# Half-size first transfers and first norms, another order of scores 4 to 7, and a last result in three parts

## The reference, cut to what matters

```python
def _L0_xattn_ref(Q, K):                      # per sequence
    scores = jnp.einsum('btd,bsd->bts', K, K) * tril
    return Q + jnp.einsum('bts,bsd->btd', scores, Q)
def _L0_ffn_ref(x, ...):
    shared = silu(x @ shared_w1.T) @ shared_w2.T            # hidden 512
    gates  = softmax of the two largest of x @ gate_w.T     # 8 experts
    selected = sum over the chosen experts of gate * (silu(x @ w1_e.T) @ w2_e.T)
    return shared + selected
x = x + tanh(g_xattn) * _L0_xattn_ref(layernorm(x), ctx)
x = x + tanh(g_ffn)   * _L0_ffn_ref(layernorm(x), ...)
```

## Time and profile before

| What | Value |
|---|---|
| median of three runs | 228.3 us |
| profiled run | 228.44 us, span 226.6 us |
| PE busy (matmul) | 220.6 us, 97% of the span |
| PEld busy (weight load, beside PE) | 191.6 us, 85% |
| DVE (VectorE) | 118.0 us, 52% |
| ACT (ScalarE) | 133.0 us, 59% |
| POOL (GpSimd) | 147.6 us, 65% |
| chain that ended last | PE 90%, DMA 3%, DVE 2%, ACT 1%, POOL 1% |
| HBM | 30.45 MB read, 12.62 MB written |

### The profile page before, as it was taken

How to read it: one execution, slowest core, us unless ns; L and a number is a source line. 1 busy time by engine, 2 the same in 40 slices (tenths; PEclk the granted TensorE clock), 3 DMA queues, 4 the chain that set the end, 5 groups by cost and what they waited for, 6 DMA issues and landing times.

```text
span 226.6 us, 5999 instructions
## 1 busy us (share of the span) xinstructions
PE 220.6 (97%) x1728; PEld 191.6 (85%) x1731; DVE 118.0 (52%) x546; ACT 133.0 (59%) x304; POOL 147.6 (65%) x178
## 2 busy tenths in 40 slices
PE   7989999999999999999999999999999999999993
PEld 2754867786777789999999999999999999999793
DVE  6899998856864589995203210221122102466214
ACT  2649896597475555655565556545654565466510
POOL 4772875767777777777777777777744544465600
PEclk9999999999999999999999999999999999999998
DMA  6899210211245995867774266777777776999633
GB/s 233 263 392 392 66 54 33 64 52 52 68 98 156 260 285 161 228 185 183 197 202 151 72 196 202 215 238 223 219 244 220 200 228 187 271 355 370 238 95 127
DMA packets 30478, 43.47 MB, mean 192 GB/s; under 512 B 4992, under 2 KB 16512, under 8 KB 30192
## 3 DMA queue, kind: packets, MB, share of 16 engines
q1 hardware_dynamic: 25264, 32.87, 49.0%
q0 software_dynamic: 4320, 9.41, 11.4%
q10 hardware_dynamic: 864, 0.80, 1.0%
HBM read 30.45 MB, written 12.62 MB: 190 GB/s over the span
## 4 chain that ended last, share of the span: by engine, by line
PE 90%; DMA 3%; DVE 2%; ACT 1%; POOL 1%; issue 1%; POOLq 0%; SPq 0%; DVEq 0%; ACTq 0%
PE bank L1343 28%; PE bank L1364 28%; PE bank L1191 11%; PE bank L1204 10%; PE bank L1317 3%; PE bank L1138 3%; PE bank L1145 2%; DMA y_rows<-y,dest 2%; PE bank L1122 2%; PE bank L1211 2%; PE bank L1155 1%; DMA q<-y_rows 1%; PE bank L1115 1%; POOL rstd L492 0%; POOL y_rows L557 0%
## 5 line engine op out<-in xcount | busy, mean ns | idle before, releaser
L557 POOL DMA_INDIRECT y_rows<-y,dest x71 | 69.7, 982 | 36.6 <-ACT y L733 25.1
L531 POOL DMA_INDIRECT expert_rows<-n,slot x64 | 62.8, 981 | 24.3 <-issue 18.3
L1364 PE MATMUL bank<-w,hT 128*128 x568 | 74.5, 275 | 0.0
L1343 PE MATMUL bank<-xT,w_ring 128*128 128x128 f32 (+1 forms) x432 | 74.1, 309 | 0.0
L1364 PEld LDWEIGHTS bank<-w,hT 128*128 128x128 f32 x568 | 71.3, 192 | 1.6
L727 ACT ACTIVATE hT<-bank 128x512 f32<-128x512 f32 x71 | 42.4, 597 | 34.3 <-PE bank L1343 34.2
L1343 PEld LDWEIGHTS bank<-xT,w_ring 128*128 128x128 f32 x432 | 59.3, 192 | 2.0 <-issue 0.2
L1024 DVE COPY xT<-bank 128x512 f32<-128x512 f32 (+2 forms) x19 | 12.4, 653 | 72.3 <-PE bank L1317 72.3
L733 ACT ACTIVATE y<-bank,gate 128x128 f32<-128x128 f32 x71 | 26.1, 368 | 21.3 <-PE bank L1364 20.9
L1204 PEld LDWEIGHTS bank<-sw,sT 128*128 128x128 f32 x224 | 27.4, 192 | 5.3 <-issue 5.0
L1191 PE MATMUL bank<-nT,sw 128*128 128x512 f32 x56 | 28.7, 609 | 0.0
(11 more groups left out here) (154 smaller groups left out, 198.1 us busy)
## 6 DMA issues: line engine op xcount, KB each, us to landing
w_ring<-in_w1T SPq DMA_DIRECT2D x54, 256.0 KB, 3.6
x_ring<-expert_rows SPq DMA_DIRECT2D x37, 72.5 KB, 2.8
x_ring<-expert_rows SPq DMA_DIRECT2D x17, 145.0 KB, 3.7
w<-in_w2T SPq DMA_DIRECT2D x2, 1024.0 KB, 11.8
kT<-y_rows SPq DMA_DIRECT2D x8, 256.0 KB, 6.5
nT<-y_rows SPq DMA_DIRECT2D x7, 256.0 KB, 4.5
out<-xres SPq DMA_DIRECT2D x7, 256.0 KB
xres<-in_xP SPq DMA_DIRECT2D x3, 512.0 KB, 7.1
```

The source lines that it names most:

```text
L531: pool.indirect_dma_start(out=x_dram[:, :], out_offset=bass.IndirectOffsetOnAxis(ap=slot[:, i, k:k + 1], axis=0), in_=n[:, i, :], in_offse ...
L557: pool.indirect_dma_start(out=y_dram[:, :], out_offset=bass.IndirectOffsetOnAxis(ap=dest[:, b:b + 1], axis=0), in_=y[:, j], in_offset=None ...
L1343: last = pe.matmul(ps_up(b)[:, j * width:(j + 1) * width], w1_ring[:, w % W_RING, c * P:(c + 1) * P], xT[:, s % X_SETS, i * P:i * P + widt ...
L1364: last = pe.matmul(ps_y(b), hidden(b, c), w2[:, ds(at + c * D, D)], start=(c == 0), stop=(c == HC - 1))
```

## The change

It touches the first 25 us and the last 4 us of the timeline. It does this:

1. The first transfers are halved: tokens of group 0 on SP, context of group 0 on ScalarE (128 KB each). `statistics1(0)` and `score(0)` start on the first half and wait for the second at their third tile.
2. VectorE no longer clears `pad`; ScalarE does, in five activations (3 pad rows of 137 columns each) after its table load.
3. GpSimd makes the identity of the scores (`ident4`) first, and TensorE waits for that alone; `keep_warm(8)` becomes `keep_warm(6)`, and the one behind `transpose_n(0)` goes.
4. `norm1(0)` and `norm2(0)` (`first_norm`) run on two columns at a time, each half released to ScalarE by itself. The constants of `positions` are made before `norm2(0)`, the other routing constants behind `norm1(2)`.
5. Scores: banks 0, 4, 7, 5, 0, 7, 0, 4; scores 4 and 7 are copied instead of 4, 5 and 6. `score(4)` stands before `apply_scores(1)`, the tiles of `score(5)` between the transposes, `score(6)` behind them, `score(7)` between `shared_up(1)` and `apply_scores(2)`. `copy_scores(4)` stands before `normalise(0)`, `copy_scores(7)` behind `shared_silu(1)`. The context of group 7 is loaded ahead of the tokens of groups 4 and 5 and of `sw2`.
6. The last result comes in three parts, two tiles, one and one, from three banks, in three stores: the first by ScalarE, the others by SP.

```diff
-        ps_s = [bank[0], bank[4], bank[7], bank[5], bank[0], bank[7], bank[4], bank[7]]
-        COPIED = (4, 5, 6)
+        ps_s = [bank[0], bank[4], bank[7], bank[5], bank[0], bank[7], bank[0], bank[4]]
+        COPIED = (4, 7)
-        ps_last_sup, ps_last_so = [bank[1], bank[2], bank[5], bank[6]], [bank[1], bank[2]]
+        ps_last_sup, ps_last_so = [bank[1], bank[2], bank[5], bank[6]], [bank[1], bank[2], bank[5]]
+        def part_of(t):
+            return max(0, t - 1)
+        def part_cols(part):
+            return slice(0, 2 * D) if part == 0 else slice((part + 1) * D, (part + 2) * D)
+        def steps_to(g, half):
+            return g + 2 if g else half + 1
...
-            load_tokens(0)
+            sp.dma_start(xres[:, 0:GW // 2], xP[:, 0:GW // 2]).then_inc(x_first, 16)
+            sp.dma_start(xres[:, GW // 2:GW], xP[:, GW // 2:GW]).then_inc(x_in[0], 16)
...
             load_context(5)
+            load_context(6)
             load_tokens(3)
             sp.dma_start(sw2[:, :], sw2T).then_inc(sw2_in, 16)
-            load_context(6)
...
-            sp.wait_ge(last_added, 2)
-            sp.dma_start(outP[:, last_cols(1)], xres[:, last_cols(1)]).then_inc(stored, 16)
-            sp.wait_ge(stored, 16 * (GROUPS + 1))
+            for part in range(1, 3):
+                sp.wait_ge(last_added, part + 1)
+                sp.dma_start(outP[:, LAST * GW:][:, part_cols(part)], xres[:, LAST * GW:][:, part_cols(part)]).then_inc(stored, 16)
+            sp.wait_ge(stored, 16 * (GROUPS + 2))
...
+            chained(pool.memset(ident4[:, :, :], 0.0))
+            pool.affine_select(out=ident4[:, :, :], ...).then_inc(ident4_ready, 1)
...
+            def norm(slot_kind, done, some=slice(0, G)):
+                slot, kind = slot_kind
+                chained(pool.tensor_tensor(rstd[:, slot, kind, some], var_eps[:, slot, kind, some], minus_half[:, some], ALU.pow))
+                pool.tensor_tensor(shift[:, slot, kind, some], neg_mean[:, slot, kind, some], rstd[:, slot, kind, some],
+                                   ALU.mult).then_inc(done, 1)
+            def first_norm(slot_kind, stats_done, done):
+                pool.wait_ge(stats_done, 1)
+                for half in range(2):
+                    norm(slot_kind, done, slice(half * G // 2, (half + 1) * G // 2))
...
-            norm1(0)
+            first_norm(first(0), stats1_done, shift1_done)
             norm1(1)
+            position_constants()
+            first_norm(second(0), stats2_done, shift2_done)
+            norm1(2)
             routing_constants()
-            norm2(0)
-            norm1(2)
             norm1(3)
...
-            act.dma_start(kT[:, 0:GW], ctxT[:, 0:GW]).then_inc(ctx_in[0], 16)
+            act.dma_start(kT[:, 0:GW // 2], ctxT[:, 0:GW // 2]).then_inc(ctx_first, 16)
+            act.dma_start(kT[:, GW // 2:GW], ctxT[:, GW // 2:GW]).then_inc(ctx_in[0], 16)
             act.preload_act_table(ACT.Silu)
+            act.wait_ge(warm_ready, 1)
+            for i in range(0, PADS, PAD_ROWS):
+                act.activation(pad[:, i:i + PAD_ROWS, 0:AT], warm[...], ACT.Copy).then_inc(pad_zeroed, 1)
...
             centre_and_scale(1, 1)
+            copy_scores(4)
             normalise(0, 0)
...
             shared_silu(0)
-            copy_scores(4)
             centre_and_scale(3, 0)
-            copy_scores(5)
             shared_silu(1)
+            copy_scores(7)
             shared_silu(2)
-            copy_scores(6)
             shared_silu(3)
...
-            chained(dve.memset(pad[:, :, :], 0.0))
...
-            def add_last_shared(half):
+            def add_last_shared(part):
+                cols = part_cols(part)
+                dve.wait_ge(half_done, GROUPS + 1 + (part > 0))
+                dve.wait_ge(sdown_done, GROUPS + part)
...
-            keep_warm(8)
+            keep_warm(6)
             score(0)
             score(1)
             score(2)
             apply_scores(0)
             score(3)
+            score(4)
             apply_scores(1)
-            score(4)
-            score(5)
-            start_score(6)
+            start_score(5)
             transpose_n(0)
-            keep_warm(1)
+            score(6)
             logit_strips(0)
             shared_up(0)
             logits(0)
             shared_up(1)
+            score(7)
             apply_scores(2)
             shared_up(2)
             positions(0)
             shared_up(3)
-            score(7)
             shared_down(0, 0)
```

More of the change, by code:

```diff
@@ L591, in normalise @@
                 if g < POWERS2:
-                    act.wait_ge(shift2_done, g + 1)
+                    act.wait_ge(shift2_done, steps_to(g, half))
                 else:
@@ L1118, in score_tile @@
             def score_tile(g, t):
+                if g == 0 and t == 0:
+                    pe.wait_ge(ctx_first, 16)
+                if g == 0 and t == G // 2:
+                    pe.wait_ge(ctx_in[0], 16)
                 for half in range(P // S):
@@ L1405, in _ @@
             for t in range(G):
-                half = t // (G // 2)
                 cols = slice(t * P, (t + 1) * P)
@@ L1410, in _ @@
                         pe.wait_ge(sT_done, HC * LAST + c + 1)
-                    last = pe.matmul(ps_last_so[half][:, cols], sT[:, LAST % 2, c, cols], sw2[:, c * D:(c + 1) * D],
+                    last = pe.matmul(ps_last_so[part_of(t)][:, cols], sT[:, LAST % 2, c, cols], sw2[:, c * D:(c + 1) * D],
                                      start=(c == 0), stop=(c == HC - 1))
-                if t % (G // 2) == G // 2 - 1:
+                if t > 0:
                     last.then_inc(sdown_done, 1)
```

46 lines of the change are left out of this document (26 added, 20 removed).

## The result

| | before | changed |
|---|---|---|
| median | 228.4 us (228.19 to 228.93, 4 runs) | 233.25 us (232.27 to 233.62, 4 runs) |
| ratio | 1 | 1.0197, 95% interval 1.0173 to 1.0220 |
| profiled run | 228.44 us, span 226.6 | 233.0 us, span 230.8 |
| score(1) starts | 6.25 | 7.76 |
| residual(0) starts | 9.71 | 13.13 |

What follows compares the result with a forecast made beforehand. The prediction took TensorE to bound the kernel, matmuls in flight 97% of the span. 228.44 + 0.15 (front) + 0 (tail) = 228.6 profiled; the profiled run stood 0.14 above the median, so 228.45, said as 228.4, range 228.0 to 228.8.

Steps and rivals of the forecast that it cites:

- Halved transfers: First loads: second halves land when the whole ones did, context 1 at 5.7, contexts 2 and 3 at 7.2.
- the upper bound: First loads: if the later issues (0.45 us each) counted, everything would land up to 0.45 later.
- a hole of 0.5: TensorE ahead of score(1): a new wait of 0.5 us for its context, until 5.7.
- rival D: TensorE's front: clock rises 3 us later after fewer warm-ups and a hole, 1.4 us in all, 229.8; chance 0.08.
- Norms in halves: GpSimd's first norms: 0.6 us per half power, first half out after 0.88 us, second after 1.8, instead of 1.32.
- rival C: GpSimd's norms: a power costs the same for two columns as for four, 1.4 us lost, 229.7; chance 0.12.
- The gain at `residual(0)`: VectorE after the first norm: residual(0) starts at 9.27 instead of 9.71, 0.44 us gained.
- The hole for the last silu: TensorE before shared_down(0, 0): idle 0.7 to 0.8 us, as score(7) no longer hides the silu.
- The clears of `pad`: ScalarE's five clears run from 4.4 to about 6.6, just in time for the first q (6.5).
- 0.88 gained and 0.15 lost: TensorE: first transpose 0.88 us earlier (13.13 for 14.01), yet shared_down(0, 0) 0.15 later (23.18 for 23.03).
- The tail: Last result in three parts, at the kernel's end: taken as 0, bounds -0.1 and +0.3 us.

Runs made afterwards that it cites:

- b_late2: Kernel before, with ScalarE waiting for one of VectorE's early memsets before issuing the context of group 1, still second on its queue: 229.29 us, 1.0039.
- b_g_first: Kernel before, with the 1 KB of gates issued first instead of third on ScalarE's queue, no halves: 231.67 us, 1.0151.
- a_filled2: Changed kernel, halved transfers kept, plus six filler matmuls behind score(0) and four before the first transpose: 231.55 us, 1.0126.
- a_whole_fill: Changed kernel with whole first transfers and four filler matmuls ahead of the first transpose: 229.85 us, 1.0043.
- a_whole: Changed kernel with the first tokens and first context loaded whole again, all else as changed: 229.75 us, 1.0023.
- a_warm8: Changed kernel with its old eight warm-up matmuls instead of six: 233.66 us, 1.0207.
- b_halves: Kernel before with the halved first transfers and their waits alone: 231.19 us, 1.0103.
- b_norms: Kernel before with the two first norms in halves and GpSimd's constants in the new order, nothing else: 228.69 us, 1.0003.
- b_scores: Kernel before with the new order of scores 4 to 7 alone: 231.02 us, 1.0112.
- b_tail: Kernel before with the last result in three parts and three stores, nothing else: 228.31 us, 0.9985.
- b_half_x: Kernel before with only the first tokens halved, on SP, the context whole: 229.46 us, 1.0035.

## Why the prediction was wrong

- **Halved transfers: the step that failed.** "The same bytes flow in the same queues, so I let the second halves land when the whole ones did", and what follows at 5.7 and 7.2, with 0.45 us as the upper bound. For the second halves it held (4.2 and 4.5). For the transfers behind them it was wrong by 2.0 us for context 1, by 2.1 for the tokens of group 1 and by 1.6 for contexts 2 and 3. The bound assumed that a later issue costs its own delay at most; b_late2 shows 1.4 for 0.41, b_g_first 2.3 for 0.48. It is the term that was mis-sized: a hole of 0.5 forecast, 2.30 measured. Putting the landings right would have added about 1.4 us at `shared_down(0, 0)` (a_filled2 less a_whole_fill), and the clock behind the hole 2.1 more.
- **The clock (rival D, 0.08).** The mechanism and its price are there, and it was given too small a chance because the hole was. The forecast hung it on two warm-ups fewer and a hole of 0.5. That alone doesn't keep the clock down: a_whole and a_whole_fill have six warm-ups and a short hole, and the clock rises at 5.9 and 4.9. With the hole at 2.30 the first rise came at 13.1. With eight warm-ups it had risen behind a hole of 1.51 (a_warm8) and was down behind one of 2.51 (b_halves). What length of hole it takes, and what the two warm-ups add, isn't shown. From that hole `score(1)` to `apply_scores(0)` run at 1.2 GHz, and `residual(0)` is 3.42 late where `score(1)` was 1.51 late. Rival D priced 3 us of late rise at 1.4; six cost about 2.
- **The second hole.** The wait ahead of the first transpose (1.07, in the variants up to 1.34) was not in the forecast: with `score(5)` gone from there nothing covers the time in which `n` is made. The forecast let the transpose simply start earlier and didn't ask what TensorE would do until then. In the changed kernel's own profiled execution the clock stays up behind it, in a_whole's, a_filled's and a_warm8's it falls, for 1.4 us and more. No claim is made of what decides between these.
- **Norms in halves: the second step that failed.** 0.70 to 0.72 us per half power, at the point (0.7) from which rival C said that the second half becomes late. Rival C itself is refuted: 128x2 isn't as long as 128x4. The gain at `residual(0)` was 0.17 in b_norms and 0.09 in a_whole_fill, for 0.44 forecast (of which a part was to come from earlier tokens), and at the first transpose 0.25 in a_whole_fill, for 0.88. The forecast also counted inside the span alone, and this edit adds 0.3 us outside it.
- **Right.** `logit_strips(0)` comes 3.00 behind the first transpose (3.02 forecast). `shared_up(3)` comes 5.15 behind that (5.16). The hole for the last silu is 0.69 (0.7 to 0.8). `start_score(0)` comes at 3.78 (3.8). The clears of `pad` take 2.29 and all but hide: the first `q` starts at 6.67, 0.2 behind its shift, in the changed kernel, and with its shift in a_whole_fill. The order of scores alone makes `shared_down(0, 0)` 0.95 late (b_scores); the forecast's 0.88 gained and 0.15 lost hold 1.03 for it.
- **The tail.** It was given -0.1 to +0.3. b_tail's median is 0.3 lower, and its interval holds the forecast's 0.

Put together: the halves alone cost 2.5 us (b_halves), all the rest without them 0.5 to 1.0 (a_whole, a_whole_fill), both together 4.8. The parts don't add up. In the profiled executions the remainder is 0.57 at `shared_down(0, 0)` (4.19, less 2.95 for the halves and 0.67 for the rest), and the clock rises at 13.1 in the changed kernel and at 11.5 in b_halves. That the shorter warm-up and the emptier stretch before the first transpose leave TensorE no cover for a late context is argued from this, not tested.

**What stays open.** Why the transfers behind a halved one land late. Packet size (b_g_first), place in the queue (b_late2) and a common shortage (b_half_x, and 78 GB/s in the last stretch) each fail as the only cause. For b_g_first and b_late2 the increments speak for the 512 KB of contexts 2 and 3: what gets behind them lands behind them. In the changed kernel context 1 is issued at 1.73 and the 512 KB at 2.18, so that isn't its cause; there two of the 16 increments of each of the three transfers above come late, and what held them the trace doesn't say. An experiment that moves the 512 KB behind the last 256 KB wasn't run. And a_filled2 lies 0.5 us above the range that I expected.

## What to carry to other kernels

The start of a kernel, in which all transfers are in flight at once, is not a place where bytes can be re-cut for free: one more issue ahead, of 1 KB or a half, or a later issue, pushed what stood behind by 1.4 to 2.4 us in these runs, so count the landing of what follows, and not of the piece you wanted sooner. When TensorE is to wait, ask what its clock will do with the hole, since it more than doubled the hole's price (2.1 us beside 1.4); and when work is moved away, look at the wait it used to cover. Try each part of such a change alone: two of its parts were worth 0.2% (1.0003 and 0.9985 by themselves, 0.9981 together), and the others hid that behind 2%.

## What the runs showed of the hardware

- A 1 KB transfer issued first lands 3.6 us after its issue, and the 256 KB behind it 4.6 and 6.3 us after theirs (b_g_first), where they took 3.8 and 4.5. Issued third, at 1.72 beside SP's 512 KB, the same kilobyte lands 5.6 us after its issue, behind all of them.
- A GpSimd power of 128x2 takes 0.70 to 0.72 us, of 128x4 1.01 to 1.04: an estimate from these two sizes is about 0.4 us fixed and 0.16 per column.
- The granted clock reads 1.00 ahead of the trace's first clock record, whatever the clock: in the changed kernel up to 13.1 us, though the identity matmul takes 0.61 at 9.36 and `apply_scores(0)` 2.08. The length of a known matmul is the better gauge there. Behind the first record the two agree (b_halves: 0.51 from 8 to 10 us, the matmul 0.61).
- The first rise of TensorE's clock isn't tied to what the kernel does alone: the identity matmul at 4.6 us takes 0.63 in the kernel before and 0.39 in b_halves, b_norms and b_scores, whose work on TensorE is the same up to there. By the clock records the first rise lies between 4.0 (b_norms) and 6.8 us (the kernel before) in all traces but the changed kernel's.
- The time outside the span isn't a constant of the chip: 1.82 to 1.93 us in every run without the halved norms and reordered constants, 2.13 to 2.23 in every run with them.
